# Window attention: where in VectorE's step the maxima of the logits stand

## The reference, cut to what matters

```python
attn = jnp.einsum('bhmc,bhnc->bhmn', q, k)
attn = fq(attn) + bias[None]
attn = fq(attn)
attn = jax.nn.softmax(attn, axis=3)
out = jnp.einsum('bhmn,bhnc->bhmc', attn, v)
out = quant_linear(out, Wout, bout)
```

## Time and profile before

| | us |
|---|---|
| median of 3 runs (5033.76 to 5056.87) | 5035.73 |
| the profiled execution | 5049.51 |
| its span, first to last instruction | 5047.8 |
| attention, start of the first A2 to start of the last, 511 steps apart | 1303.5 to 2440.0 |
| mean granted TensorE clock over the span, 1 being 2.4 GHz | 0.901 |

### The profile page before, as it was taken

How to read it: one execution, slowest core, us unless ns; L and a number is a source line. 1 busy time by engine, 2 the same in 40 slices (tenths; PEclk the granted TensorE clock), 3 DMA queues, 4 the chain that set the end, 5 groups by cost and what they waited for, 6 DMA issues and landing times. The chain is left out here.

```text
span 5047.8 us, 116742 instructions
## 1 busy us (share of the span) xinstructions
PE 4034.7 (80%) x40394; PEld 2558.1 (51%) x40394; DVE 3893.2 (77%) x7098; ACT 3248.6 (64%) x5602; POOL 1485.4 (29%) x1812
## 2 busy tenths in 40 slices
PE   1686777676698988988566669996689999999999
PEld 1233554444577777777455434443345454554544
DVE  7797999999999999989655410002799999999985
ACT  0675777775698988989466544443656666666664
POOL 0201111111667666766522200001132222212210
PEclk9997777876899999999777779997799999999999
DMA  8773666665333333333277778885122222222212
GB/s 319 208 216 106 161 160 164 166 165 133 81 96 95 91 95 92 95 87 99 83 274 268 274 250 289 288 288 177 47 73 95 74 90 82 74 93 83 90 56 68
DMA packets 270448, 725.18 MB, mean 144 GB/s; under 512 B 30602, under 2 KB 177290, under 8 KB 252362
## 3 DMA queue, kind: packets, MB, share of 16 engines
q1 hardware_dynamic: 259466, 675.31, 45.2%
q0 software_dynamic: 10560, 44.53, 2.2%
HBM read 428.25 MB, written 291.50 MB: 143 GB/s over the span
## 5 line engine op out<-in xcount | busy, mean ns | idle before, releaser
L861 POOL TENSOR_TENSOR exp_lo<-exp,exp_hi 128x294 f16<-128x294 f32 x1024 | 788.6, 798 | 358.1 <-ACT exp_hi L932 354.4
L1646 PE MATMUL out_psum<-gelu_hi,w_parts 128*128 128x448 f16 x2016 | 605.1, 355 | 58.7 <-DVE w_parts L1822 31.5
L1682 ACT ACTIVATE gelu_pair<-h_psum,b_rows,w_unscale 128x448 f32<-128x448 f32 x448 | 324.6, 728 | 413.1 <-PE h_psum L1598 224.9
L1718 DVE BATCH_NORM_STATS2 ln_stats<-z_img 128x6 f32<-128x192 f32 x448 | 126.0, 344 | 562.4 <-DMA z_img<-zd 561.7
L1382 PE MATMUL conv_psum<-c_in,toeplitz 128*128 128x448 f16 (+1 forms) x2304 | 470.2, 366 | 64.9 <-DMA dwb<-in_L_conv_dw_b_dram 62.4
L1598 PE MATMUL h_psum<-ln_parts_T,w_hi 128*128 128x448 f16 x2016 | 494.8, 355 | 17.5 <-DVE w_in L1781 15.7
L957 DVE SCALAR_TENSOR_TENSOR logit_int<-attn_int,scalars,bias_products 128x588 f16<-128x588 int8 x512 | 486.6, 951 | 13.1 <-issue 9.8
L1646 PE MATMUL out_psum<-gelu_lo,w_parts 128*128 128x448 f16 x1344 | 475.5, 354 | 0.0
L938 ACT ACTIVATE attn_int<-p_psum,scalars 128x588 int8<-128x588 f32 x512 | 386.3, 755 | 133.1 <-PE p_psum L464 131.2
L619 PE MATMUL range_psum<-q_diag,k_diag 128*128 128x196 bf16 x1536 | 275.6, 316 | 227.7 <-DVE p_min L701 224.9
L911 PE MATMUL o_psum<-a_v,exp_hi 128*128 128x34 f16 x6144 | 383.1, 179 | 77.9 <-DVE a_o L984 58.0
(11 more groups left out here) (313 smaller groups left out, 9879.9 us busy)
## 6 DMA issues: line engine op xcount, KB each, us to landing
k_diag<-kd SPq DMA_DIRECT2D x128, 384.0 KB, 5.1
toeplitz<-gd SPq DMA_DIRECT2D x48, 1024.0 KB, 17.1
yd<-y_out SPq DMA_DIRECT2D x16, 2880.0 KB, 27.2
c_in<-yd SPq DMA_DIRECT2D x24, 1920.0 KB, 9.4
zd<-c_out POOLq DMA_DIRECT2D x24, 1792.0 KB, 13.8
z_img<-zd SPq DMA_DIRECT2D x16, 2688.0 KB, 9.4
x_chunk<-in_x_dram SPq DMA_DIRECT2D x12, 3136.0 KB, 10.9
x_img<-in_x_dram SPq DMA_DIRECT2D x16, 2352.0 KB, 15.9
```

The costliest lines, as they stand in the source:

```text
L861: last = nc.gpsimd.tensor_tensor(el[r][:, :, 2 * a, 0:N], src[:, :, a], eh[r][:, :, 2 * a, 0:N], ALU.subtract)
L1646: last = nc.tensor.matmul(po[:, t, 0:TCH], w, hx[:, f, cols], start=f == 0 and x == 0, stop=f == NF - 1 and x == len(steps) - 1)
L1682: nc.scalar.activation(h[y // 2 % 3][:, y % 2], ph[:, y % 3, 0:TCH], ACT.Gelu, scale=k1[:], bias=b1[:, f:f + 1]).then_inc(hd, 1)
```

## The change

VectorE's MX stage goes from the end of its step to the head. Its waits, its pair number and the instruction are as before; it issues no transfer. No lag is changed, and no other engine's list.

```diff
             def step(n, l, stage):
+                if stage(LAG_MX):
+                    m, r = n - LAG_MX, (l - LAG_MX) % 4
+                    dve.wait_ge(td, m + 1)
+                    if stage(LAG_MX + 4):
+                        dve.wait_ge(lgd, m - 3)
+                    v.tensor_reduce(nmx[r][:], pt[:, 0:5].rearrange("p c (w n) -> p c w n", w=2)[:, :, :, 0:N], AX.X, ALU.max,
+                                    negate=True).then_inc(mxd, 1)
                 if stage(LAG_A2):
                     m, r = n - LAG_A2, (l - LAG_A2) % 4
                     dve.wait_ge(a1d, m + 1)
...
                     v.tensor_tensor(dst, src, rr, ALU.mult).then_inc(nrm, 1)
-                if stage(LAG_MX):
-                    m, r = n - LAG_MX, (l - LAG_MX) % 4
-                    dve.wait_ge(td, m + 1)
-                    if stage(LAG_MX + 4):
-                        dve.wait_ge(lgd, m - 3)
-                    v.tensor_reduce(nmx[r][:], pt[:, 0:5].rearrange("p c (w n) -> p c w n", w=2)[:, :, :, 0:N], AX.X, ALU.max,
-                                    negate=True).then_inc(mxd, 1)
```

## The result

The changed kernel takes 5865.76 us in the median of 3 runs (5864.6 to 5866.45) against 5035.73: 1.1612 times as long, 95% interval 1.158 to 1.1645. The forecast was 5872, range 5690 to 6040.

The account below looks back on a forecast made before the run. Before, three engines were close to full, none alone setting the pace; after, a closed VectorE-TensorE loop would. 505 x (3.83 - 2.224) = 811 us plus 25 of stalls, on 5036, gave 5872 us, range 5690 to 6040.

Parts of the forecast that it names:

- MX is due one step earlier, with the order around VectorE's cycle the same: In VectorE's attention steps, N(m-6) instead of N(m-5) stands ahead of MX(m); the order stays N, MX, A2, R, S.
- The loop N, PV, QK, T, MX, A2, R, S, N: In the attention, VectorE and TensorE run these one behind the other, closing every step, about 505 steps; 0.62 with mixed clock.
- Its length: One step of the attention loop: 1.88 + 1.67 = 3.55 us at 2.4 GHz, 4.12 us at 1.2 GHz.
- The clock: TensorE, idle 1.57 us of each attention step, was to run about half the time at 1.2 GHz, half at 2.4.
- another stage: The stage of the product ranges, taken as nearest to a steady case: no TensorE idle time over 1.7 us, clock 0.74.
- that rival: The attention loop with the clock at 2.4 GHz throughout: 3.55 us a step, 5731 us; chance 0.17.
- The stalls and the mean step: Attention stalls, four ends of loop bodies and other waits, 0 to 54 us, taken as 25; mean step 3.83 us.
- the step at the mixed clock: Attention step taken as 3.83 us, the middle of 3.55 and 4.12, against 2.224 before: 811 us over 505 steps.
- The 836 us: Forecast growth of the kernel: 811 us from 505 longer attention steps plus 25 us of stalls, put on 5036.
- A2 at 0.82 us: VectorE's A2 in the attention loop taken at its undisturbed time; 1.06 in every step would add 121 us.

Follow-up runs that it names:

- experiment 6: The kernel before with MX moved up one place only, from behind N to ahead of it: 5227.29 us, ratio 1.036.
- experiment 2: The changed kernel with A2 moved from behind MX to behind N: 5386.76 us, ratio 1.0678.
- experiment 1: The changed kernel with PV one step later, lag 7 in place of 6: 5115.48 us, ratio 1.0126.
- experiments 7 and 8: The changed kernel with S issued twice, the copy into a scratch column: ahead of N (7) 6029.72 us, behind N (8) 5859.11 us.
- experiment 5: The changed kernel with four extra matmuls of 256 columns ahead of L in each step, their result overwritten: 5750.62 us, ratio 1.1396.
- experiment 3: The kernel before with PV one step later, MX still at the end of its step: 5654.0 us, ratio 1.1193.

## Why the prediction was right, by its own steps

- **MX is due one step earlier, with the order around VectorE's cycle the same.** Shown by experiment 6, which moves MX by a single place and gets the step of that loop, with PV at most 0.15 us behind N's end in every step, and by the waits after the change.
- **The loop N, PV, QK, T, MX, A2, R, S, N.** Shown from several sides. Taking A2 out of it makes a step of 2.81 us (experiment 2), taking PV out ends it (experiment 1), a term added to it counts in full, and a term added beside it not at all (experiments 7 and 8).
- **Its length.** 3.55 at 2.4 GHz and 4.12 at 1.2 were worked out; 3.55 and 4.10 stand in the timeline, and they are the medians of the steps at either level. Each term came from a row of before in which that hand-over happened to be waited for once.
- **The clock.** A mean of 0.74 was taken from another stage, 0.77 was measured. That TensorE's idle time of each step brings the clock down is shown by experiment 5: with 0.43 us of the 1.57 filled, the clock is 0.99 and the time 115 us less. The forecast of that rival was 5731 and the filled kernel takes 5751. That 0.74 came so near is in part luck: nothing on record says why the two stages should be alike, and other loops here held 0.71 (experiment 7), 0.92 (experiment 3) and 0.99 (experiment 2). By the rule in the Trainium skill (TensorE: Matmul & The Clock Gate, HAM oscillation — how this bites in real kernels) the clock would have stayed at 2.4 GHz but for the ends of the loop bodies, for about 5731. The trace does not agree: TensorE's idle times in the loop are 1.9 us at most, with four of 4.5 to 4.6 us at the ends of loop bodies, and yet the mean clock of the phase is 0.77.
- **The stalls and the mean step.** The stalls were sized about right. The steps at the four ends of loop bodies take 8.80 to 8.88 us, some 21 us more than four of 3.55, and with the clock held at 0.99 in experiment 5 the mean step is (3140.4 - 1299.9) / 511 = 3.602, that is 26 us over 511 steps of 3.55. The term that was mis-sized is the step at the mixed clock: with those 21 us taken out of the 1948.1 the mean is 3.77 us, not 3.83. So the span grew by 815 us where 836 were forecast.
- **The hit at 6 us is in part luck.** The 836 us were put on the median before, 5036, while the profiled execution of the kernel before was 14 us over that median and the one after 1 us under its own. That took back 15 of the 21 us. Put on the 5050 to 5056 us that the kernel before took in the later sessions, the same 836 would have forecast 5886 to 5892, 20 to 26 us over the measured time.
- **A2 at 0.82 us.** Right: the median is 0.821 after with a mean of 0.82, and 0.831 before with a mean of 0.95. What stretched A2 was left unnamed, and it stays open; the last section says what the runs show of it.
- **What was missed stands outside that sum:** in the control of experiment 3 I took a lag for a neutral edit and overlooked the mirrored loop through `t_psum`.

## What to carry to other kernels

When an instruction moves over the boundary of a step in a software-pipelined loop, write the new cycle with pair numbers, not with stage names: the order of the names here stayed the same and only the number changed. Then look for a closed chain that alternates between two engines. There can be one through each single buffer, that is, for each wait of the kind "the reader has finished". Where such a chain is longer than any engine's own list, its length is the step, and it is read off the trace of before, hand-over by hand-over. In this kernel MX was free where its producer, T, stood in TensorE's list ahead of the PV that waits for the N just done, and the step became as long as the chain where T stood behind that PV.

## What the runs showed of the hardware that I had not expected

- Useless matmuls can pay: four of 256 columns in each step took the phase's granted clock from 0.77 to 0.99 and 115 us off the kernel; ten of them had the same clock and only some 22 us, which is hardly more than the shift between sessions.
- A2 and GpSimd's subtraction, with the two laid over one another in experiment 1, took 1.24 to 1.30 us and 1.94 us for the pair of instructions, in place of 0.82 and 1.41. GpSimd's timeline there:

```profile
1999.91 1.94 POOL L861 TENSOR_TENSOR exp_lo<-exp,exp_hi 128x294 f16<-128x294 f32 x2 [0.43 <-ACT exp_hi L932]
```

- That GpSimd's work lies over A2 is not enough, though. In experiment 3 it begins during nearly every A2, and the median A2 keeps its 0.82 us; there GpSimd's pair takes 1.72:

```profile
2003.11 0.82 DVE L957 SCALAR_TENSOR_TENSOR logit_int<-attn_int,scalars,bias_products 128x588 f16<-128x588 int8 x1
...
2003.49 1.72 POOL L861 TENSOR_TENSOR exp_lo<-exp,exp_hi 128x294 f16<-128x294 f32 x2 [1.51 <-ACT exp_hi L932]
```

In the long A2 shown here, of experiments 1 and 5, GpSimd had begun first (1999.91 against 2000.03, 2004.15 against 2005.08); in the short one of experiment 3 A2 had (2003.11 against 2003.49). No experiment moved the one against the other alone, so that the order decides is not shown.
